# Pacing the scatters of the routing loop by value products, and fewer idle matmuls before the experts

## The chip, the cores and the metric

The kernel runs on one core of one Trainium2 chip. The metric is the device time of one launch in microseconds (us), the median of several runs. A profile of one execution gives, for each engine, when every instruction began and ended and what it waited for. The engines are TensorE (PE, its weight loads PEld), VectorE (DVE), ScalarE (ACT), GpSimd (POOL) and SyncE (SP, which issues most transfers).

## What is computed

Two transformer layers on an input of 8 samples x 512 tokens x 128 features, each with an attention part and a feed-forward part around which a layer norm and a modulation by a condition vector stand. What matters here is layer 0. Its attention goes through 16 heads of 8 features; its feed-forward part sends each token to 4 of 16 experts:

```python
logits = -dist2 + jnp.einsum('bld,ed->ble', x, rw) + rb
topv, topi = jax.lax.top_k(logits, TOP_K)          # 4 of 16 experts per token
w = jax.nn.softmax(topv, axis=-1)
hidden = jax.nn.gelu(jnp.einsum('bld,efd->blef', x, w1) + b1, approximate=False)
exp_out = jnp.einsum('blef,edf->bled', hidden, w2) + b2
fused = jnp.sum(w[..., None] * sel, axis=2)        # the 4 chosen, weighted
```

Every expert has a 128x512 and a 512x128 matrix. Layer 1 follows with another attention and a spiking feed-forward part; the change leaves both alone.

## The kernel before

**The loop over samples (`layer0_attention`).** The work on a sample is cut into a front (projections, and fifteen steps d = 1 to 15 of a recurrence) and a back (scores, softmax, value products). A pass of the loop does the back of sample b and the front of sample b + 1, and, from the second sample on, also the routing of sample b - 1. In the first pass (sample 0's back) there is no routing; then come six passes of one `Fori` loop on each engine, and a last one without a front.

The order of instructions on each engine is a string: `weave(order, b=..., f=..., r=...)` takes the next piece of the back for a `b`, of the front for an `f` and of the routing for an `r`. `ORDER_ROUTE` holds these strings for the six passes: `'pe'`, `'ve'`, `'act'` and `'po'`. An engine runs its instructions strictly in the order of its string, and waits at each for the semaphores that it needs.

**What POOL does in a pass.** Of the recurrence, step d is: VectorE multiplies (L831, L837, tiles `a_tU`, `a_txy`), TensorE sums over heads (L1121, L1129), VectorE multiplies the result (L850, L855), and POOL subtracts it from `a_K` (L456, one instruction) and `a_X` (L462, two). The next step needs these. The steps shrink: 128x480 elements at d = 1, 128x32 at d = 15.

In the routing of sample b - 1, `route_pool` issues sixteen scatters, one for each of 4 token tiles and 4 chosen experts (L1573): each writes 128 token rows of 130 numbers (67 KB) from `a_mats` to places in DRAM (`rows_h`) given by a list of indices. POOL issues them between the steps of the recurrence, where its string has an `r`.

**What TensorE does meanwhile.** The back's last part runs over 40 jobs (sample tile, head group, tile of keys): scores (L1301, L1310, L1313), an exponential on ScalarE (L664) and the value products (L1325, eight matmul instructions of one job in the trace). The event `e_pv` counts jobs whose value products are done: `e_pv(k)` is reached after job k.

**The end of a pass.** VectorE writes fourteen 128x512 products of the front to `a_mats` (L872). The tenth and later overwrite the rows that the scatters read, so ahead of them VectorE waits until all sixteen scatters have landed (`R.sent`). POOL waits for the same before it says that its pass is over. Then SyncE clears the semaphores and starts the next pass.

**The last routing and the experts (`layer0_experts`).** The routing of the last sample stands outside the loop. TensorE has six short pieces in it (`route_tensor`); between and behind them it runs idle matmuls (`warm`, L207: a 128x128 constant times itself into an unused bank; one `w` is one f32 matmul, which the trace shows as two matmul instructions). The string is `'w' * 7 + 'rwww' * 7 + 'w' * 80`. Meanwhile SyncE loads the weights of all experts (16 x 514 KB) and small tables, and POOL issues the last sixteen scatters.

Then 143 pages of 128 rows follow, each one expert's: SyncE waits until all scatters have landed (L1821) and loads page p from `rows_h` (L1826, 65 KB, up to ten ahead); TensorE transposes it (L1960), VectorE copies the transposed page (L1935), TensorE multiplies by the first matrix (L1968), ScalarE applies gelu (L1853), TensorE multiplies by the second (L1977), VectorE scales (L1943), POOL scatters the result (L1838). The product L1968 runs two pages behind L1960, and L1977 three. TensorE's instructions for the pages stand behind all idle matmuls.

## Time and profile before

| | us |
|---|---|
| median of 3 runs | 2345.96 |
| lowest and highest | 2341.86, 2352.36 |
| the profiled execution, time | 2352.26 |
| the profiled execution, span from first to last instruction | 2350.1 |
| TensorE busy | 2055.5 (87%) |
| VectorE busy | 1644.5 (70%) |
| ScalarE busy | 869.7 (37%) |
| GpSimd busy | 836.0 (36%) |
| mean granted TensorE clock | 0.903 (no unit) |

The profiled execution lies 6.3 us above the median and 2.16 us above its own span. A value of 1.00 for the granted clock means that TensorE ran at its higher level (2.4 GHz) all through a stretch, 0.50 that it ran at the lower one (1.2 GHz).

How to read it: the busy shares are an average over stages. The stages are, in us from the start of the span: set-up and sample 0's front to some 200; the back of sample 0 to 312 (its last value product); the six passes with routing, whose last value products end at 499.8, 687.5, 875.2, 1067.0, 1258.2 and 1449.3; the last back to 1645; the last routing to 1694; the expert pages to 1969; layer 1 to the end.

### The profile page before, as it was taken

The page shows a single profiled execution, that of the slowest core. Times are in us where ns is not written, and L with a number is a line of the kernel's source. Part 1 is how long each engine was busy: PE and PEld are TensorE (multiplying, and loading weights), DVE is VectorE, ACT ScalarE, POOL GpSimd, SP SyncE. Part 2 cuts the span into 40 slices and gives each one's busy share as a digit, 9 for nine tenths or more (in the row PEclk, how much of TensorE's full clock was granted, in tenths as well). Part 3 has the DMA queues.
Part 4 walks back from the last instruction along what each step waited for, and adds up shares of the span by engine and source line. Part 5 has one row for each costly group of instructions (what it writes and reads, how often), then busy time and mean ns, then how long its engine had stood idle before and what let it go on. Part 6 is the DMA issues. An engine that isn't in the chain of part 4 may idle for free. (4 is left out here: it accounts for less than half of the span.)

```text
span 2350.1 us, 44343 instructions
## 1 busy us (share of the span) xinstructions
PE 2055.5 (87%) x16519; PEld 1373.3 (58%) x16519; DVE 1644.5 (70%) x3673; ACT 869.7 (37%) x1694; POOL 836.0 (36%) x871
## 2 busy tenths in 40 slices
PE   4798998988988898898898899989799999788885
PEld 2573564564555465456456456766799998345443
DVE  5968759839938947856874883540366765999996
ACT  2022233223224234133222322312166653887782
POOL 1523413622532532451352254130366653222211
PEclk7898999989989989889898888987899999899997
DMA  3000000000000000000000000120622223100000
GB/s 108 10 3 15 1 2 15 11 12 15 4 19 15 1 20 17 1 20 3 14 13 10 15 4 18 37 97 1 238 72 72 72 71 90 49 18 28 5 9 14
DMA packets 70189, 72.63 MB, mean 31 GB/s; under 512 B 12976, under 2 KB 58592, under 8 KB 69840
## 3 DMA queue, kind: packets, MB, share of 16 engines
q1 hardware_dynamic: 61296, 51.75, 7.4%
q0 software_dynamic: 8672, 17.91, 2.2%
q8 instruction: 142, 2.33, 0.4%
q14 instruction: 79, 0.65, 0.1%
HBM read 38.05 MB, written 27.43 MB: 28 GB/s over the span
## 5 line engine op out<-in xcount | busy, mean ns | idle before, releaser
L664 ACT ACTIVATE a_prep<-ps 128x1536 f32<-128x1536 f32 (+1 forms) x112 | 155.6, 1389 | 349.8 <-PE ps L1310 207.3
L905 DVE TENSOR_REDUCE a_mpart<-ps 128x4 f32<-128x512 f32 x320 | 199.6, 683 | 56.8 <-PE ps L1251 33.7
L1853 ACT ACTIVATE b_hid<-ps,b_stage 128x128 f32<-128x128 f32 x572 | 162.8, 368 | 143.9 <-PE ps L1968 132.0
L1838 POOL DMA_INDIRECT rows_y<-b_orow,b_target x143 | 164.7, 1152 | 123.9 <-DVE b_orow L1943 120.6
L462 POOL TENSOR_TENSOR a_X<-a_X,a_txy 128x480 f32<-128x480 f32 (+14 forms) x240 | 180.9, 771 | 64.5 <-DVE a_txy L855 63.3
L456 POOL TENSOR_TENSOR a_K<-a_K,a_yU 128x480 f32<-128x480 f32 (+14 forms) x120 | 83.7, 697 | 331.0 <-DVE a_yU L850 329.8
L1129 PE MATMUL ps<-a_txy,cst 128*128 128x480 f32 (+14 forms) x480 | 181.7, 485 | 11.0 <-DVE a_txy L837 10.3
L1977 PE MATMUL ps<-b_stage,b_hid 128*128 128x128 f32 x1144 | 151.4, 276 | 1.5 <-ACT b_hid L1853 1.5
L1968 PE MATMUL ps<-b_hTp,b_stage 128*128 128x128 f32 x1144 | 151.2, 275 | 0.0
L207 PE MATMUL ps<-cst 128*128 128x128 f32 x862 | 133.7, 303 | 15.8 <-issue 10.3
L872 DVE TENSOR_TENSOR a_mats<-ps,cst 128x512 f32<-128x512 f32 x112 | 69.9, 684 | 100.9 <-PE ps L1158 100.9
L1977 PEld LDWEIGHTS ps<-b_stage,b_hid 128*128 128x128 f32 x1144 | 139.3, 192 | 2.0 <-ACT b_hid L1853 2.0
L207 PEld LDWEIGHTS ps<-cst 128*128 128x128 f32 x862 | 119.8, 212 | 33.9 <-issue 30.7
L1968 PEld LDWEIGHTS ps<-b_hTp,b_stage 128*128 128x128 f32 x1144 | 139.0, 192 | 0.0
L1573 POOL DMA_INDIRECT rows_h<-a_mats,r_slot x112 | 111.1, 992 | 72.4 <-DVE a_mpart L905 47.9
L1121 PE MATMUL ps<-a_tU,cst 128*128 128x480 f32 (+14 forms) x240 | 92.3, 469 | 41.0 <-DVE a_tU L831 40.6
L1129 PEld LDWEIGHTS ps<-a_txy,cst 128*128 128x128 f32 x480 | 86.4, 216 | 67.9 <-issue 40.1
L837 DVE TENSOR_TENSOR a_txy<-a_bw,a_X 128x480 f32<-128x480 f32 (+14 forms) x240 | 110.8, 484 | 20.7 <-POOL a_X L462 20.4
L855 DVE TENSOR_TENSOR a_txy<-a_wf,ps 128x480 f32<-128x480 f32 (+14 forms) x240 | 94.7, 416 | 40.4 <-PE ps L1129 39.6
L1247 PE MATMUL ps<-a_aux_g,a_g_hotb 24*128 24x512 bf16 (+1 forms) x320 | 94.9, 415 | 27.2 <-DVE a_mpart L905 20.9
L1325 PE MATMUL ps<-a_prep,a_values 128*32 128x128 f32 x2560 | 116.8, 306 | 1.7 <-issue 1.7
L1325 PEld LDWEIGHTS ps<-a_prep,a_values 128*32 128x32 f32 x2560 | 69.4, 120 | 64.9 <-issue 56.0
(467 smaller groups left out, 4578.5 us busy)
## 6 DMA issues: line engine op xcount, KB each, us to landing
b_hrow<-rows_h SPq DMA_DIRECT2D x143, 65.0 KB
b_w<-in_wexp SPq DMA_DIRECT2D x16, 514.0 KB
d_got<-rows_y SPq DMA_DIRECT2D x32, 256.0 KB, 4.0
rows_h<-a_txy SPq DMA_DIRECT2D x19, 325.0 KB
rows_y<-b_orow,b_target POOLq DMA_INDIRECT x143
out<-xs SPq DMA_DIRECT2D x8, 256.0 KB, 2.3
cst<-in_const SPq DMA_DIRECT2D x1, 1865.5 KB, 15.0
rows_h<-a_mats,r_slot POOLq DMA_INDIRECT x112
```

Of the source, the lines that this page charges most:

```text
L207: nc.tensor.matmul(out, square, square, start=True, stop=True, skip_group_check=True)
L462: nc.gpsimd.tensor_tensor(x, x, yX[:, a, 0:n].rearrange("p (c s) -> p c s", c=NC), ALU.subtract).then_inc(e_uX.sem, 1)
L664: nc.scalar.activation(Pt[:, at:at + width, :], ps[:, 4:4 + width, :], ACT.Exp).then_inc(e_exp.sem, width)
L837: nc.vector.tensor_tensor(by_chunk(tX[:, a, 0:n]), chunks(bw[:, :])[:, :, left], chunks(X2[:, a, :])[:, :, right], ALU.mult).then_inc(e_tX ...
L905: nc.vector.tensor_reduce(mpart[:, i, j, 4 * g:4 * g + 4], ps[:, 4 + n % 4, :].rearrange("p (r j) -> p r j", r=4), AX.X, ALU.max).then_inc ...
L1129: mm(ps[:, 1 + a, 0:n], con("block8"), tX[:, a, 0:n], start=True, stop=True).then_inc(e_pX.sem, 1)
L1325: last = mm(ps[32 * r:32 * r + 32, 7, 128 * g:128 * g + 128], vflat[:, v0:v0 + 32], Pt[:, at, 128 * r:128 * r + 128], start=j == i and g = ...
L1573: nc.gpsimd.indirect_dma_start(hrows, bass.IndirectOffsetOnAxis(R.slot[:, t, k:k + 1], 0), R.htok[:, t, k, :], None).then_inc(R.scattered, 16)
L1838: nc.gpsimd.indirect_dma_start(yrows, bass.IndirectOffsetOnAxis(target[:, p % DEEP:p % DEEP + 1], 0), orow[:, p % DEEP, :], None).then_inc ...
L1853: last = nc.scalar.activation(hid[:, p % 2, f, :], ps[:, p % 2, 128 * f:128 * f + 128], ACT.Gelu, bias=stage[:, p % 3, AT_B1 + f:AT_B1 + f ...
L1968: last = mm(ps[:, q % 2, 128 * f:128 * f + 128], stage[:, q % 3, 128 * f:128 * f + 128], hTp[:, q % 2, :], start=True, stop=True, skip_gro ...
L1977: last = mm(ps[:, 4 + r % 2, 0:D], hid[:, r % 2, f, :], stage[:, r % 3, F + D * f:F + D * f + D], start=f == 0, stop=f == NF - 1, skip_gro ...
```

## The change

Two edits. In the loop, `route_pool` gets a list of sixteen events: scatter n now also waits for `e_pv(2 * n + 1)`, the value products of job 2n + 1. With it POOL's string is another. Behind the last routing, 24 idle matmuls stand in place of 80.

```diff
@@ ORDER_ROUTE @@
-    'po': ('bbbbbbbfffffffffffffffbfffbfbbbfbbfbbffffffffffffrfrffrfrffrfrffrfrrfffrrrrrr'),
+    'po': ('bbbbbbbfffffffffffffffbfffbfbbbfbbfbbffffffffffffrfffrrfffrrffrfrfrffrfffrrrrrrr'),
@@ layer0_attention, POOL @@
-                both(b + 2, ORDER_ROUTE, b, r=route_pool(nc, po, R, V, hrows))
+                both(b + 2, ORDER_ROUTE, b, r=route_pool(nc, po, R, V, hrows, pace=[e_pv(2 * n + 1) for n in range(16)]))
@@ layer0_experts, TensorE @@
-            weave('w' * 7 + 'rwww' * 7 + 'w' * 80, r=route_tensor(nc, pe, ps, cst, R, V), w=warm(nc, ps[:, 7, 0:128], ident))
+            weave('w' * 7 + 'rwww' * 7 + 'w' * 24, r=route_tensor(nc, pe, ps, cst, R, V), w=warm(nc, ps[:, 7, 0:128], ident))
```

`route_pool` itself is unchanged; it already waits for `pace[4 * t + k]` ahead of each scatter where a list is given, as in the pass behind the loop.

On POOL, in a pass of the loop, from the first scatter on. L1573 is a scatter, L456 and L462 are the recurrence's subtractions (128x32xN is step 16 - N). Before:

```order
L1573 DMA rows_h<-a_mats,r_slot 77824x130
L456 TENSOR_TENSOR a_K<-a_K,a_yU 128x32x5
L1573 DMA rows_h<-a_mats,r_slot 77824x130
L462 TENSOR_TENSOR a_X<-a_X,a_txy 128x32x5 x2
L1573 DMA rows_h<-a_mats,r_slot 77824x130
L456 TENSOR_TENSOR a_K<-a_K,a_yU 128x32x4
L1573 DMA rows_h<-a_mats,r_slot 77824x130
L462 TENSOR_TENSOR a_X<-a_X,a_txy 128x32x4 x2
L1573 DMA rows_h<-a_mats,r_slot 77824x130
L456 TENSOR_TENSOR a_K<-a_K,a_yU 128x32x3
```

The same place after the change:

```order
L1573 DMA rows_h<-a_mats,r_slot 77824x130
L456 TENSOR_TENSOR a_K<-a_K,a_yU 128x32x5
L462 TENSOR_TENSOR a_X<-a_X,a_txy 128x32x5 x2
L1573 DMA rows_h<-a_mats,r_slot 77824x130 x2
L456 TENSOR_TENSOR a_K<-a_K,a_yU 128x32x4
L462 TENSOR_TENSOR a_X<-a_X,a_txy 128x32x4 x2
L1573 DMA rows_h<-a_mats,r_slot 77824x130 x2
L456 TENSOR_TENSOR a_K<-a_K,a_yU 128x32x3
```

At steps 11 and 12 the two subtractions from `a_X` now stand ahead of the scatter that stood ahead of them. At the end of the list six scatters stood behind the last step of the recurrence before, and seven stand there now. The other engines' lists are the same in the loop.

On TensorE, behind the last routing (L1764 is the last piece of the routing, L1960 the first transposes of pages), the difference of the two programs:

```order
 L207 MATMUL ps<-cst 128x128 x3
 L1764 MATMUL ps<-b_b,b_flat 128x128 x4
-L207 MATMUL ps<-cst 128x128 x86
+L207 MATMUL ps<-cst 128x128 x30
 L1960 MATMUL ps<-cst,b_hrow 128x128 x3
 L1968 MATMUL ps<-b_hTp,b_stage 128x128 x4
```

Six of the 86 come from the pieces `www` of the string, so 30 are left in place of 86, and nothing else moves.

## Rows read from the trace of the kernel before

**Rows 1.** Busy time by stretch: engines, granted clock, DMA share, GB/s; passes of the loop.

```profile
687.50:875.20 187.70, 166.97 (x1529) 102.14 (x1529) 135.87 (x310) 55.93 (x84) 72.55 (x83) 0.91 0.04 12
875.20:1067.00 191.80, 171.29 (x1529) 104.24 (x1529) 135.78 (x310) 55.82 (x84) 72.92 (x83) 0.88 0.04 11
...
687.50:816.30 128.80, 109.75 (x837) 67.57 (x838) 109.76 (x224) 37.05 (x68) 47.23 (x46) 0.92 0.03 8
875.20:1008.00 132.80, 114.05 (x838) 69.51 (x838) 109.59 (x224) 37.05 (x68) 47.42 (x46) 0.88 0.03 8
```

**Rows 2.** Timeline of POOL in the sixth pass: start, us, instruction, idle time before.

```profile
1412.73 0.87 POOL L462 TENSOR_TENSOR a_X<-a_X,a_txy 128x128 f32<-128x128 f32 x2
...
1419.04 0.98 POOL L1573 DMA_INDIRECT rows_h<-a_mats,r_slot  x1 [0.17 <-issue]
...
1432.80 0.96 POOL L1573 DMA_INDIRECT rows_h<-a_mats,r_slot  x1 [0.31 <-issue]
1462.09 0.61 POOL L465 COPY a_vown<-a_vf 128x512 f32<-128x512 f32 x1 [28.33 <-SPq L404]
```

**Rows 3.** Timeline of VectorE in the same pass.

```profile
1413.23 0.67 DVE L837 TENSOR_TENSOR a_txy<-a_bw,a_X 128x96 f32<-128x96 f32 x2 [1.38 <-POOL a_X L462]
...
1453.53 1.89 DVE L872 TENSOR_TENSOR a_mats<-ps,cst 128x512 f32<-128x512 f32 x3 [1.56 <-PE ps L1158]
```

**Rows 4.** Timeline of TensorE in the same pass.

```profile
1415.64 0.42 PE L1325 MATMUL ps<-a_prep,a_values 128*32 128x128 f32 x8
...
1425.98 0.39 PE L1301 MATMUL ps<-a_aux_g,a_aux_l 32*128 32x512 bf16 x3 [1.09 <-ACT a_prep L664]
...
1429.81 1.51 PE L1325 MATMUL ps<-a_prep,a_values 128*32 128x128 f32 x24
...
1435.40 1.51 PE L1325 MATMUL ps<-a_prep,a_values 128*32 128x128 f32 x24
...
1438.96 0.86 PE L1325 MATMUL ps<-a_prep,a_values 128*32 128x128 f32 x24
```

**Rows 5.** Busy time by stretch again: behind the last routing, and the pages.

```profile
1700.00:1950.00 250.00, 249.10 (x2234) 248.91 (x2233) 175.43 (x542) 149.69 (x527) 151.90 (x132) 1.00 0.25 71
1660.90:1669.70 8.80, 8.80 (x78) 8.79 (x78) 3.21 (x16) 0.00 (x0) 6.19 (x7) 1.00 1.02 407
1669.70:1684.30 14.60, 4.38 (x15) 3.09 (x14) 1.45 (x2) 0.00 (x0) 9.24 (x10) 0.62 0.98 338
1684.30:1694.50 10.20, 10.16 (x81) 10.15 (x81) 0.00 (x0) 0.00 (x0) 0.00 (x0) 0.88 0.21 48
```

**Rows 6.** Timeline behind the last routing, 1660 to 1696 us, all engines.

```profile
1680.73 0.96 POOL L1573 DMA_INDIRECT rows_h<-b_htok,r_slot  x1 [0.31 <-issue]
...
1695.27 0.30 PE L1960 MATMUL ps<-cst,b_hrow 128*128 128x128 f32 x1 [0.37 <-DVE b_hTp L1935]
...
1695.41 1.12 PE L1968 MATMUL ps<-b_hTp,b_stage 128*128 128x128 f32 x8
```

**Rows 7.** Timeline of SyncE's queue between 1684 and 1700 us.

```profile
1685.99 10.17 SPq L1826 DMA_DIRECT2D b_hrow<-rows_h  x10
```

**Rows 8.** Busy time by stretch of 1 us while the first pages land.

```profile
1686.00:1687.00 1.00, 1.00 (x7) 1.00 (x7) 0.00 (x0) 0.00 (x0) 0.00 (x0) 0.61 0.11 21
1687.00:1688.00 1.00, 1.00 (x11) 1.00 (x11) 0.00 (x0) 0.00 (x0) 0.00 (x0) 1.00 0.26 61
...
1689.00:1690.00 1.00, 1.00 (x11) 1.00 (x11) 0.00 (x0) 0.00 (x0) 0.00 (x0) 1.00 0.32 67
```

**Rows 9.** The idle matmuls (L207) between 1660.9 and 1694.6 us: count, durations in ns.

```profile
L207 PE MATMUL ps<-cst x172: 268/276/556, 1660.9 to 1694.4; 128*128 128x128 f32 x172
```

**Rows 10.** Another start of TensorE after a pause, at layer 1: timeline, then busy time.

```profile
1976.30 11.69 PE L207 MATMUL ps<-cst 128*128 128x128 f32 x88 [3.28 <-PEq L1773]
```

**Rows 11.** Busy time by stretch: the start of that burst.

```profile
1976.90:1980.30 3.40, 3.40 (x18) 3.40 (x18) 1.14 (x1) 1.44 (x5) 0.00 (x0) 0.50 0.95 269
```

**Rows 12.** DMA queues between 1660 and 1663 us: packets, MB, share of 16 engines.

```profile
q8 instruction: 1, 0.02, 2.1%
```

More of the change, by code:

```diff
@@ L163 @@
            'rffbffrffrfffffffbfffffffffffffffffffffbffffffffffffffbbbbbbfffbbbfffbb'),
-    'po': ('bbbbbbbfffffffffffffffbfffbfbbbfbbfbbffffffffffffrfrffrfrffrfrffrfrffrrfffrrrrrr'),
+    'po': ('bbbbbbbfffffffffffffffbfffbfbbbfbbfbbffffffffffffrfffrrfffrrffrfrfrffrfffrrrrrrr'),
 }
```

## Prediction

> **What bounds the kernel now.** I read the page's busy shares first: TensorE is busy for 87% of the span and its granted clock averages 0.903. So in most stages TensorE's own list sets the pace, and an engine beside it can be late without cost. Then I read the two places that the change touches.
>
> In the loop, the busy times by stretch [rows 1] show two kinds of pass. From the last value product of one sample to that of the next it takes 187.7 us in the second and third pass and 191.8, 191.2 and 191.1 in the next three. The scores and value products, which are the part with the scatters, take the same in both kinds: 875.2 - 816.3 = 58.9 us and 1067.0 - 1008.0 = 59.0. The rest takes 128.8 or 132.8 us, at a granted clock of 0.92 or 0.88. So the 3.5 us between the kinds lie outside the part with the scatters and are clock. In that part TensorE is all but never idle: its longest pause in the sixth pass is 1.09 us, and ScalarE's exponential ends it, not POOL or VectorE [rows 4].
>
> Behind the last routing, the stretches [rows 5] show three phases of TensorE: dense idle matmuls to 1669.7, then 14.6 us in which only 15 matmuls and 14 loads ran while the DMA engines were full (0.98), then 81 dense ones to 1694.5. The first pages stand behind them, and the pages are bound by TensorE from there on: 249.1 us busy in 250.
>
> **The loop, part by part.** A scatter costs POOL 0.96 to 1.0 us, before and after; nothing is added there but sixteen waits in POOL's queue. Scatter n waits for job 2n + 1. What is queued behind a waiting scatter is the next subtraction of the recurrence, for which VectorE and then TensorE wait.
>
> Do the waits hold? The tightest of the scatters between the steps is the eighth. It starts at 1419.04 [rows 2], and its job 15 is the eight products that begin at 1415.64 and end at 1416.06 [rows 4]: 3.0 us in hand. The others of the first twelve have 3 us or more. From the thirteenth on the waits do hold: jobs 25, 27, 29 and 31 lie in the groups of three jobs (24 products each) that end at 1431.3, 1436.9 and 1439.8 [rows 4]. The last scatter moves from 1432.80 [rows 2] to about 1439.7, which is 6.9 us. Behind these four POOL has nothing to do: they are the last of its pass, and it then stands idle for 28.33 us until the next pass at 1462.09 [rows 2].
>
> Who waits for their landing? VectorE before the tenth product into `a_mats`, the second of the three from 1453.53, so 1454.2 [rows 3]. The landing itself: where the DMA engines were full, a scatter begun at 1680.73 [rows 6] was down when SyncE went on at 1685.99 [rows 7], 5.3 us; in the loop, with a DMA share of 0.04 [rows 1], it should be less. 1439.7 + 5.3 = 1445.0 leaves 9 us. Cost: 0, and if that cover were gone, what is later than 1454.2 would count in full, six times.
>
> The moved order gives something back off the path: at step 12 the subtractions from `a_X` stood behind a scatter, began at 1412.73 [rows 2], and VectorE stood idle 1.38 us for them [rows 3]; step 11 is alike. They now go first, about 1 us earlier. TensorE was not waiting for it, since its list was full there, so I count 0. The bounds: nothing below, and 1 us for each of two places in six passes, 12 us, if TensorE did feel them; I take 0, because its only pause over 1 us there has another cause [rows 4].
>
> **The idle matmuls.** 86 matmuls are 172 instructions [rows 9], 56 fewer matmuls are 112 fewer. Dense, one takes 8.80 / 78 = 0.113 us [rows 5], so the 60 that are left end at 1660.9 + 6.8 = 1667.7, before the thin phase begins. TensorE then waits for pages.
>
> The pages come as before, because SyncE's first load does not depend on TensorE: it goes out at 1685.99, the ten within 10.17 us [rows 7]. The stretches of 1 us [rows 8] show 61 KB in 1687 to 1688 and 67 in 1689 to 1690, with the same between; a page is 65 KB, so three are down at 1690.0. The third transpose, from which the list of the pages runs without a gap, begins at 1695.27 with the first product at 1695.41 [rows 6]. It can begin at 1690.0: 5.3 us earlier.
>
> Off this goes the clock. Now the idle matmuls raise it before the pages: their second burst starts at 1684.34 and the stretch 1686 to 1687 has 0.61, which is the lower level until 1686.8, so 2.4 us into the burst [rows 8]. At layer 1 a burst that starts at 1976.30 after a pause of 3.28 us runs at 0.50 up to 1980.3 at least, 4.0 us [rows 10, 11]. After the change the pages themselves are that burst. At the lower level TensorE does half, so 2.4 to 4.0 us cost 1.2 to 2.0. If the gaps of a starting pipeline kept the level low for 8 us it would be 4.0; if TensorE were not slowed at all, 0. I take 1.6, the middle of the two measured starts.
>
> The sum: 5.3 - 1.6 = 3.7 us, between 1.3 and 5.3. It passes whole through the pages, which TensorE bounds. The profiled execution should come from 2352.26 (span 2350.1) to 2348.6 (2346.4); that execution is 6.3 us above the median, and against the median it is 2345.96 - 3.7 = **2342.3 us**.
>
> The Trainium skill, in "TensorE: Matmul & The Clock Gate", section "What's actually happening", says that the throttled state is the default and that activity releases it. That rule speaks against this edit, since idle matmuls are such activity; by itself it gives the 1.2 to 2.0 us that the rows above have, and no more.
>
> **Rivals.**
>
> *The thin phase exists only under the profiler.* For it: in the 14.6 us TensorE took an instruction every 0.5 us (15 and 14, rows 5), while POOL went on issuing a scatter every 1.3 us, and a block of TensorE's instructions came in during the full phase of the DMA engines [rows 12]. So neither a lack of instructions nor of data explains it. Without the thin phase the 172 instructions end at 1660.9 + 172 x 0.113 = 1680.3, 8 us before the first page, and the 56 matmuls were free in every timed run. Then the time is 2345.96, no change, and only the profile gets shorter. Against it: the phase begins and ends with the DMA load (338 GB/s, then 48), and the profiled execution is no slower than the slowest timed one (2352.26 against 2352.36).
>
> The Trainium skill has two rules on this. "NOTIFIC — the notification-queue block", section "Overflow: three behaviours, one of which stalls the engine", says that the block which writes trace records holds its producer up rather than lose a record inside it. "Runtime: NRT & Kernel Launch", section "Instruction fetch mechanics", says that TensorE holds 2048 instructions, refilled in blocks of 256. Both are for this rival; no row here shows either.
>
> *The loop's passes change their kind for the better.* Three of six profiled passes are of the long kind. All six at 187.7 would take 4.1 + 3.5 + 3.4 = 11.0 us off the profiled execution; but the median is already 6.3 below it, so about 4.7 are left: 2342.3 - 4.7 = 2337.6. For it: VectorE's work moves by a microsecond in each pass. Against: that is not where the kinds differ [rows 1].
>
> *The passes go to the long kind.* The mechanism is the clock in the front's part of a pass: 132.8 in place of 128.8 us, at 0.88 [rows 1]. All six long are 6 x 3.5 = 21 us above all short, the median is 4.7 above all short, so 16.3 are left to lose: 2342.3 + 16.3 = 2358.6, slower than before. It decides when one more stretch of a pass falls to the lower level, as it did from the fourth pass on with no change at all in the program.
>
> *A paced scatter holds up the recurrence.* That needs the value products to come 3.0 us later against POOL's list than now [rows 2, 4]. Every further microsecond then delays a subtraction and TensorE behind it in six passes: at 2 us over, 12 us, 2354. Nothing moves TensorE's list in the loop, so this is unlikely.
>
> **How the numbers follow.** Forecast 0.45 (2340.7 to 2344.7); thin phase only under the profiler 0.32 (2346); short passes 0.11; long passes 0.08; held recurrence 0.04. The runs before lie 10.5 us apart, which is three passes of the other kind, so each case is blurred by some 4 us. A range of 2336 to 2352 leaves out the last two cases and the far end of the short passes, about 2 in 10. A measurement tells some 0.5% from no change, 11.7 us: faster than 2334.2 needs short passes and more, 0.07; slower than 2357.7 is the upper end of the long passes, 0.05; within it 0.88.
>
> **What would show it.** In the profile after: 60 idle matmul instructions behind the last piece of the routing, ending near 1667.7 on the old scale, no thin phase, the first transposes 6 us nearer to the routing's end than now (1688 on the old scale), a low clock at the first two pages. In the loop: the last scatter some 7 us later, VectorE's waits for `a_X` of 1.4 us gone, the value part still 58.9 us. I am wrong if the pages start later than 3 us before their old place, if the value part changes, or if VectorE waits for landed scatters. If the profile gains 3.7 us and the timed runs nothing, the first rival has it.

## The result, and the profile after

The changed kernel takes 2376.4 us (median of 4, 2364.4 to 2383.5) against 2344.6 for the kernel before in the same comparison (median of 4): ratio 1.0125, 95% interval 1.0073 to 1.0177. It is slower by 1.2%, where 2342.3 us and no measurable change were forecast. The profiled execution takes 2383.5 us with a span of 2381.4, 31.3 more than before. (Ratios leave out runs over 1.5% above the fastest of their kernel and medians keep them, which shows in e9, where one of four is left out, and in e16, three of ten.)

From the page of the changed kernel, the row of busy times:

```profile
PE 2068.6 (87%) x16407; PEld 1370.8 (58%) x16407; DVE 1648.6 (69%) x3673; ACT 871.1 (37%) x1694; POOL 836.6 (35%) x871
```

TensorE has 112 instructions fewer and is busy 13.1 us longer. The mean granted clock of the profiled execution is 0.889 (0.903 before).

**The loop.** Busy time by stretch of the changed kernel, with the columns of [rows 1]: the third of the six passes, its front's part, its part with scores and value products, and a piece of that.

```profile
700.10:900.60 200.50, 179.02 (x1529) 108.48 (x1529) 136.60 (x310) 55.94 (x84) 72.92 (x83) 0.85 0.04 11
700.10:831.10 131.00, 111.22 (x834) 67.89 (x838) 109.90 (x224) 37.07 (x68) 47.28 (x46) 0.91 0.03 8
831.10:900.60 69.50, 67.80 (x707) 40.58 (x695) 26.71 (x87) 18.87 (x16) 25.64 (x38) 0.73 0.05 17
...
854.60:888.70 34.10, 34.10 (x282) 21.06 (x282) 4.76 (x20) 9.29 (x7) 12.89 (x20) 0.50 0.06 20
```

The same 1529 matmuls now take 200.5 us, against 187.7 or 191.8 in [rows 1]. The front's part, 131.0 us, lies between the two known lengths (128.8 and 132.8); the value part, the scores and value products, took 58.9 us in every pass before and has grown by ten. In one piece of 34.1 us TensorE is busy without a gap, but at a granted clock of 0.50. (Below, a value part is counted from the start of its first product: 59.5 us for each pass before.) The six value parts of the changed kernel take 60.7, 64.4, 69.8, 69.8, 69.9 and 59.5 us: 37.4 more in all. The front's parts take 5.4 more. The last sample, whose code is unchanged, gives 9.4 back, again by the clock. The first of these rows is the kernel before, the second the one after:

```profile
1449.30:1636.10 186.80, 168.37 (x1627) 121.27 (x1623) 68.57 (x165) 44.20 (x62) 36.21 (x37) 0.86 0.12 43
```

```profile
1492.20:1669.60 177.40, 162.28 (x1624) 117.19 (x1623) 68.32 (x165) 44.23 (x62) 36.28 (x37) 0.89 0.13 45
```

What stands ahead of the low clock, in the sixth pass of the changed kernel: the timelines of TensorE, ScalarE and POOL (start, us, instruction, idle time before).

```profile
1449.56 1.43 PE L1310 MATMUL ps<-a_shared,a_roll_k 32*16 32x64 f32 x42
1450.92 0.96 PE L1325 MATMUL ps<-a_prep,a_values 128*32 128x128 f32 x22
1452.17 0.40 PE L1325 MATMUL ps<-a_prep,a_values 128*32 128x128 f32 x2 [0.29 <-issue]
...
1454.51 0.39 PE L1301 MATMUL ps<-a_aux_g,a_aux_l 32*128 32x512 bf16 x3 [1.07 <-ACT a_prep L664]
```

```profile
1453.01 1.45 ACT L664 ACTIVATE a_prep<-ps 128x1536 f32<-128x1536 f32 x1 [4.74 <-PE ps L1325]
```

```profile
1450.15 1.05 POOL L1573 DMA_INDIRECT rows_h<-a_mats,r_slot  x1 [0.16 <-issue]
1451.51 0.96 POOL L1573 DMA_INDIRECT rows_h<-a_mats,r_slot  x1 [0.30 <-issue]
```

The exponential waits for the matmuls L1310, which end at 1450.99; it begins 2.0 us after that. (The view names L1325, whose matmuls had ended when the report came; the step of L1310's own semaphore is recorded 1.94 us behind the last of them. Such a step, by which an engine tells the others that it is done, is called a report below.) In those 2 us stand two scatters in a row, which the new order has at step 11. TensorE halts 0.29 us in the middle of the value products, for nothing that the profile shows, and then 1.07 us for the exponential. The pause of 1.09 us in [rows 4] is the same thing. The rows of ScalarE and POOL around it, in the kernel before:

```profile
1424.48 1.45 ACT L664 ACTIVATE a_prep<-ps 128x1536 f32<-128x1536 f32 x1 [3.78 <-PE ps L1325]
```

```profile
1421.63 0.99 POOL L1573 DMA_INDIRECT rows_h<-a_mats,r_slot  x1 [0.16 <-issue]
1422.92 0.96 POOL L1573 DMA_INDIRECT rows_h<-a_mats,r_slot  x1 [0.30 <-issue]
```

The L1310 of these jobs end at 1422.50, so this exponential too is 2.0 us late, and here it is the ninth and tenth scatter that stand in a row. The pause ends 34.6 us into the value part in the first three passes and 36.1 in the last three. After the change it ends at 20.4 to 24.5 us. Behind the second pair of the new order, at step 12, TensorE does not halt; in the first and the last pass a further pause of 0.94 us ends 48 to 49 us into the value part, among the last scatters.

**POOL and VectorE.** The last scatter of the sixth pass, and what follows on POOL; then VectorE's first product on `a_X` at step 13:

```profile
1482.79 0.96 POOL L1573 DMA_INDIRECT rows_h<-a_mats,r_slot  x1 [1.47 <-PE ps L1325]
1504.95 0.61 POOL L465 COPY a_vown<-a_vf 128x512 f32<-128x512 f32 x1 [21.21 <-SPq L404]
```

```profile
1455.11 0.68 DVE L837 TENSOR_TENSOR a_txy<-a_bw,a_X 128x96 f32<-128x96 f32 x2
```

The waits hold from the thirteenth scatter on, and POOL still stands idle for 21.21 us behind them (28.33 in [rows 2]). VectorE no longer waits for `a_X` here (1.38 us in [rows 3]); over the whole kernel these waits of L837 sum to 3.2 us in place of 20.4. The products into `a_mats` wait for TensorE's L1158 (1.56 us ahead of the three from 1496.40, as in [rows 3]), and not for scatters.

**The pages.** TensorE behind the last routing, then the clock at the first pages:

```profile
1693.36 6.96 PE L207 MATMUL ps<-cst 128*128 128x128 f32 x60
1722.37 0.45 PE L1960 MATMUL ps<-cst,b_hrow 128*128 128x128 f32 x1 [22.05 <-DMA b_hrow<-rows_h]
...
1724.42 0.47 PE L1960 MATMUL ps<-cst,b_hrow 128*128 128x128 f32 x1 [0.56 <-DMA b_hrow<-rows_h]
1724.68 1.91 PE L1968 MATMUL ps<-b_hTp,b_stage 128*128 128x128 f32 x8
```

```profile
1722.30:1728.40 6.10, 4.91 (x21) 4.35 (x22) 1.68 (x7) 1.14 (x4) 0.00 (x0) 0.50 0.28 65
1728.40:1735.00 6.60, 6.60 (x61) 6.60 (x61) 4.29 (x14) 4.17 (x15) 3.43 (x3) 1.00 0.25 62
```

In both programs one can count from the end of the routing's matmuls: the third transpose comes at 31.0 us against 34.3 before, the last at 298.7 against 300.6: 1.9 us gained.

### The profile page after: what moved, and what is told of

It is laid out like the page before. It is cut to its first block and busy times, and to the rows that moved or that the text cites. A ratio compares the mean times of both kernels' runs of the same rounds, so it can differ in the third digit from the quotient of the medians.

```text
span 2381.4 us, 44119 instructions
## 1 busy us (share of the span) xinstructions
PE 2068.6 (87%) x16407; PEld 1370.8 (58%) x16407; DVE 1648.6 (69%) x3673; ACT 871.1 (37%) x1694; POOL 836.6 (35%) x871
## 5 line engine op out<-in xcount | busy, mean ns | idle before, releaser
L456 POOL TENSOR_TENSOR a_K<-a_K,a_yU 128x480 f32<-128x480 f32 (+14 forms) x120 | 83.7, 698 | 371.0 <-DVE a_yU L850 370.1
L462 POOL TENSOR_TENSOR a_X<-a_X,a_txy 128x480 f32<-128x480 f32 (+14 forms) x240 | 181.6, 772 | 83.8 <-DVE a_txy L855 82.0
L1129 PE MATMUL ps<-a_txy,cst 128*128 128x480 f32 (+14 forms) x480 | 187.9, 500 | 13.8 <-DVE a_txy L837 13.0
L1573 POOL DMA_INDIRECT rows_h<-a_mats,r_slot x112 | 110.7, 988 | 101.3 <-DVE a_mpart L905 47.0
L872 DVE TENSOR_TENSOR a_mats<-ps,cst 128x512 f32<-128x512 f32 x112 | 69.9, 683 | 104.0 <-PE ps L1158 104.0
L1325 PE MATMUL ps<-a_prep,a_values 128*32 128x128 f32 x2560 | 123.0, 316 | 1.8 <-issue 1.7
L207 PE MATMUL ps<-cst 128*128 128x128 f32 x750 | 115.1, 299 | 5.4 <-PEq L1773 3.2
L207 PEld LDWEIGHTS ps<-cst 128*128 128x128 f32 x750 | 102.1, 207 | 23.4 <-issue 20.2
L837 DVE TENSOR_TENSOR a_txy<-a_bw,a_X 128x480 f32<-128x480 f32 (+14 forms) x240 | 110.3, 482 | 3.5 <-POOL a_X L462 3.2
L1325 PEld LDWEIGHTS ps<-a_prep,a_values 128*32 128x32 f32 x2560 | 72.1, 123 | 67.4 <-issue 56.6
```

What stands on the lines that cost most here:

```text
L207: nc.tensor.matmul(out, square, square, start=True, stop=True, skip_group_check=True)
L462: nc.gpsimd.tensor_tensor(x, x, yX[:, a, 0:n].rearrange("p (c s) -> p c s", c=NC), ALU.subtract).then_inc(e_uX.sem, 1)
L837: nc.vector.tensor_tensor(by_chunk(tX[:, a, 0:n]), chunks(bw[:, :])[:, :, left], chunks(X2[:, a, :])[:, :, right], ALU.mult).then_inc(e_tX ...
L1129: mm(ps[:, 1 + a, 0:n], con("block8"), tX[:, a, 0:n], start=True, stop=True).then_inc(e_pX.sem, 1)
L1325: last = mm(ps[32 * r:32 * r + 32, 7, 128 * g:128 * g + 128], vflat[:, v0:v0 + 32], Pt[:, at, 128 * r:128 * r + 128], start=j == i and g = ...
L1573: nc.gpsimd.indirect_dma_start(hrows, bass.IndirectOffsetOnAxis(R.slot[:, t, k:k + 1], 0), R.htok[:, t, k, :], None).then_inc(R.scattered, 16)
```

## The experiments

Each of the five groups of experiments ran on one chip, another for each group, and before was timed beside it. Theory 1 was that scatters in a row make reports between engines late, that TensorE pauses for it, and that the clock goes down after a pause there. Rivals: the waits in POOL's queue, the missing idle matmuls, the chip, chance.

### The parts alone (e1 to e4)

e1_idle24:

```diff
-            weave('w' * 7 + 'rwww' * 7 + 'w' * 80, r=route_tensor(...
+            weave('w' * 7 + 'rwww' * 7 + 'w' * 24, r=route_tensor(...
```

> The kernel before with twenty-four idle matmuls in place of eighty behind the last routing, and nothing else; the loop is as before. In the profile after, the pages' first transpose stands 29.0 us behind the start of the last row of idle matmuls (1693.36 to 1722.37) against 33.6 us before (1660.9 to 1694.5), and the last transpose 298.7 against 300.6 us: 1.9 us earlier. If the pairs of scatters or the waits in the loop made the changed kernel slower, this one is 1 to 4 us faster than before (ratio 0.998 to 1.000), with passes of 187.7 and 191 us. If the idle matmuls keep the clock up for what follows, it carries part of the loss: 2350 to 2376. If the thin phase exists only under the profiler, the profiled span is 2 to 4 us shorter and the timed runs do not move.

e2_order (the changed string of POOL, without waits):

```diff
-    'po': ('...ffffffffffffrfrffrfrffrfrffrfrffrrfffrrrrrr'),
+    'po': ('...ffffffffffffrfffrrfffrrffrfrfrffrfffrrrrrrr'),
```

> The kernel before with the changed order of the scatters in the loop alone; no scatter waits for value products, eighty idle matmuls. Theory 1 (pairs): a scatter that starts right behind another holds up the reports between the engines for some 2.4 us, TensorE pauses and ScalarE's exponential begins 2 us late; the new order makes such pairs at the steps 11 and 12, some 13 us earlier in the value part, and the clock falls there. Then this kernel carries all or most of the loss: value parts of 64 to 69 us in place of 58.9, passes of 198 to 201, time 2370 to 2385. Theory 2 (waits): the loss comes from scatters that stand in POOL's queue waiting, or land late; then this kernel takes 2340 to 2350. Theory 3 (both needed): in between, 2350 to 2368.

e3_waits (the waits, with the string of before):

```diff
-                both(b + 2, ORDER_ROUTE, b, r=route_pool(nc, po, R, V, hrows))
+                both(b + 2, ORDER_ROUTE, b, r=route_pool(nc, po, R, V, hrows, pace=[e_pv(2 * n + 1) for n in range(16)]))
```

> The kernel before with the sixteen waits on value products alone; the order of the scatters is that of before. The waits bind from the thirteenth scatter on. Theory 1 (pairs): the only pair between the steps is the one of before (the ninth and tenth), so nothing is lost: 2338 to 2352, perhaps a little less, since the row of six at the end is spread out. Theory 2 (waits): it carries the loss, 2370 to 2385. A mixture of both gives 2352 to 2368.

e4_apart (no scatter behind another between the steps; at the end of the list the eleventh and twelfth still begin 1.3 to 2.1 us apart):

```diff
-    'po': ('...ffffffffffffrfrffrfrffrfrffrfrffrrfffrrrrrr'),
+    'po': ('...ffffffffffffrfrffrfrffrfrffrfrffrfrffrrrrrr'),
...
+                ... pace=[e_pv(n) for n in (1, 1, 1, 1, 1, 1, 1, 1, 1, 1, 1, 24, 27, 30, 33, 36)]))
```

> The kernel before with no two scatters in a row: the tenth goes behind the subtraction of step 15, and the last five wait for the value products of jobs 24, 27, 30, 33 and 36; eighty idle matmuls. Theory 1 (pairs): the pause of the value products with the ninth and tenth scatter (0.28 us inside a group, then 1.09 us before the scores) goes, and with it the fall of the clock behind it; the value part comes under 58.9 us, by 1.4 us at least in each of six passes and by up to 5 us if the clock stays up for the 10 to 14 us that it is down now: 2315 to 2338. Theory 2 (waits): it has as many binding waits as the changed kernel and loses as much: 2365 to 2385. If the clock's pattern comes of other things, value parts stay at 58.9 and the time at 2340 to 2350.

Measured, against 2308.4 us for before (31 runs, 2286.8 to 2335.8): e1 2306.9, ratio 1.0018 [0.9976, 1.0060]; e2 2309.1, 0.9996 [0.9954, 1.0038]; e3 2309.5, 1.0013 [0.9965, 1.0062]; e4 2312.7, 1.0014 [0.9971, 1.0056]. No part moves the time, and keeping scatters apart gains nothing either. The times of 2338 us and more that the theories gave are all missed, because before itself is 36 us faster here than in the first comparison, which I had not expected. The value part of e2, with the pairs of the changed order in it, and one of e4:

```profile
1187.20:1243.40 56.20, 55.81 (x708) 33.94 (x707) 27.31 (x88) 18.86 (x16) 25.75 (x38) 0.91 0.07 21
```

```profile
1189.30:1241.00 51.70, 51.11 (x708) 31.70 (x707) 26.73 (x87) 18.76 (x16) 25.28 (x38) 1.00 0.07 21
```

e2 shows no pause behind its pairs. 51.7 us is what a value part takes if the clock never falls. So either order and waits are slow only together, or the chip is a condition. The parts were not run again on a chip like that of the first comparison.

### The whole change on another chip (e5 to e8)

e5_before is the kernel before, e6_changed the changed kernel, e7_loop the changed loop with eighty idle matmuls. e8_late:

```diff
-    'po': ('...ffffffffffffrfrffrfrffrfrffrfrffrrfffrrrrrr'),
+    'po': ('...fffffffffffffffffffffffffffrrrrrrrrrrrrrrrr'),
```

> The kernel before once more, unchanged, for a profile of it beside those of the changed parts on the same chip. In the first comparison it took 2344.6 us and its value parts 59.4; among the runs of the parts it took 2308.4, and none of the four profiles there (e1 to e4) had a report of TensorE more than 1.0 us late, where the two first profiles had such in every pass (up to 1.9 us behind a pair of scatters). Theory 1 (the chip, not the program): here its value parts take 52 to 56 us and the scatters hold up no reports, if the time is near 2308; or 59.4 us with late reports, if it is near 2345. Theory 2 (chance of one execution): value parts of both kinds within runs of one call, and no link between late reports and time.

> The changed kernel, whole. Theory 1 (late reports behind pairs of scatters, on some chips alone): where before takes near 2308 us, it is 0 to 3 us faster than before or the same (ratio 0.997 to 1.001), with value parts of 52 to 56 us; where before takes near 2345 us, it is 1.2% slower again, with the pause of 1.1 us some 20 us into the value part. Theory 2 (the order and the waits together cost time on any chip, though neither does alone): 1.2% slower here too, 2330 to 2340 against 2308.

> The changed loop (order and waits) with the eighty idle matmuls of before. Theory 1: as the changed kernel in the loop, and 1.9 us slower than it behind the last routing. Where the changed kernel is 1.2% slower than before, this one is too, and the idle matmuls have no part in the loss; where it is not, this one is within 0.3% of before. If the idle matmuls were the cause, this kernel would be at before's time while the changed one is slower.

> The kernel before with all sixteen scatters of a pass behind the last step of the recurrence, in one row of some 20 us (from 1426 to 1447 on the scale of before), so that none lies in the first 36 us of the value part and fifteen stand right behind another. Theory 1, on a chip with late reports: the pause of 1.1 us at the ninth and tenth scatter goes, the first 36 us of the value part get shorter by 1.4 us or more, and late reports come in the row behind it; the time is 2320 to 2360 by how the clock takes it. On a chip without: the same as before within 0.3%, and no report late. If a row of scatters costs time on any chip, 10 us or more over before.

Measured, against 2309.5 (31 runs): e5 2311.6, 0.9974 [0.9940, 1.0008]; e6 2309.6, 0.9979 [0.9940, 1.0017]; e7 2307.8, 1.0003 [0.9963, 1.0042]; e8 2301.3, 0.9974 [0.9939, 1.0009]. The whole change makes no difference here, and sixteen scatters in one row (e8) cost nothing. From e6: the value part of the fifth pass by stretch, and in the sixth TensorE's L1310, the exponential of the same jobs as above and the pair of scatters.

```profile
1187.10:1243.10 56.00, 55.58 (x707) 33.77 (x699) 27.09 (x87) 18.86 (x16) 25.57 (x38) 0.91 0.07 21
```

```profile
1391.71 1.43 PE L1310 MATMUL ps<-a_shared,a_roll_k 32*16 32x64 f32 x42
```

```profile
1393.25 1.45 ACT L664 ACTIVATE a_prep<-ps 128x1536 f32<-128x1536 f32 x1 [2.84 <-PE ps L1310]
```

```profile
1392.32 1.05 POOL L1573 DMA_INDIRECT rows_h<-a_mats,r_slot  x1 [0.16 <-issue]
1393.67 0.96 POOL L1573 DMA_INDIRECT rows_h<-a_mats,r_slot  x1 [0.30 <-PE ps L1325]
```

The 42 matmuls L1310 end at 1393.14 here and the exponential begins 0.1 us later, with the same two scatters around it. So scatters in a row are not enough to make a report late. With each report of TensorE in the loop set against the end of its matmul, none of e1 to e15 is more than 0.3 us behind; in the first comparison L1310's is 1.9 us behind at this place in each of the six passes of both kernels. The page of e5 also shows which chip it is, in its list of transfers:

```profile
b_hrow<-rows_h SPq DMA_DIRECT2D x143, 65.0 KB, 1.9
b_w<-in_wexp SPq DMA_DIRECT2D x16, 514.0 KB, 10.2
```

The last number is the time from issue to landing. The pages of the first comparison have none for these two, because many landings are missing from those traces. Counted from the traces, 5053 and 5070 reports lie behind the last value product in before and after, and over 8600 in every trace of e1 to e15; in the front's parts, where nothing is scattered, the numbers are the same (916 in most). The time between the two kinds of chip lies in the same places. The span of before is 2350.1 us in the first comparison and 2310.2 in e5; of these 39.9 us, 29.6 are in the six value parts, 11.3 in the last sample and 5.1 between the routing's end and the last transpose of a page, while the front's parts are 5.8 us shorter in the first comparison.

And the idle matmuls in e5, from the end of the routing to the first page:

```profile
1627.34 19.47 PE L207 MATMUL ps<-cst 128*128 128x128 f32 x172
1654.14 0.45 PE L1960 MATMUL ps<-cst,b_hrow 128*128 128x128 f32 x1 [7.33 <-DMA b_hrow<-rows_h]
```

There is no thin phase. All 172 instructions are through in 19.47 us, and TensorE then waits 7.33 us for the page. In e1 to e15 the last transpose comes 295.3 to 297.0 us behind the routing, with either number of idle matmuls.

### A pause made on purpose (e9 to e12)

Is the pause the cause of the low clock, or another sign of the chip? e9_late12 makes it on a chip without late reports:

```diff
+        aside = sb("aside", [128, 6, 208], BF16)
...
                     at, width = LANES * (k % 2), len(group)
+                    if k in late:
+                        for n in range(6):
+                            nc.scalar.activation(aside[:, n, :], ps[:, 4, 0:208], ACT.Exp)
                     nc.scalar.activation(Pt[:, at:at + width, :], ps[:, 4:4 + width, :], ACT.Exp).then_inc(e_exp.sem, width)
...
+                weave(order['act'], b=back((4,) if routing else ()), f=front(nxt, True), **routing)
```

e10_late24 has `(8,)` there. e11_changed_late12 is the changed kernel with `(4,)`, and e12_changed the changed kernel.

> The kernel before, with six small activations on data nobody uses (some 1.8 us) ahead of ScalarE's exponential of the jobs 12 to 14 in the loop. In the changed kernel's first trace that exponential began 2 us late, TensorE stood 1.1 us for it some 22 us into the value part, and 1.8 us later its clock fell for 34 us; on the two chips of the runs e1 to e8 none of the three was there. Theory 1 (a pause of TensorE at this place makes the clock fall and stay low; where the pause comes from does not matter): the clock falls at 23 to 27 us into the value part for 17 to 34 us, value parts of 60 to 70 us in place of 53 to 56, 6 x 7 to 14 = 40 to 80 us over before. Theory 2 (the fall had another cause, such as the chip): the pause costs itself at most, 1 to 2 us a pass, 6 to 12 us over before (ratio 1.003 to 1.005), and the clock keeps its pattern.

> The same six activations ahead of the exponential of the jobs 24 to 26, where the first trace of the kernel before had the pause (34.6 us into the value part, and the clock fell there for 13.6 us; on the other chips it falls at the same place for 6.8 or 10.2 us, or not at all, without a pause). Theory 1: the value parts of the first trace of before come back, 58 to 60 us in every pass, 20 to 35 us over before (ratio 1.009 to 1.015), and less than e9. Theory 2: 6 to 12 us.

> The changed kernel with the six activations ahead of the exponential of the jobs 12 to 14. Theory 1: as e9, value parts of 60 to 70 us. If the new order of the scatters behind the pause is what holds the clock low, it is above e9 by 10 us or more; if the pause alone does it, within 8 us of e9. Theory 2: 6 to 12 us over the changed kernel.

> The changed kernel once more, beside the other three, for a third chip if it is one. On a chip like those of e1 to e8 (before near 2308 us, no report over 1 us late) the ratio to before is 0.994 to 1.002; on one like the first (before near 2345, reports up to 1.9 us late behind a pair of scatters) it is 1.007 to 1.018 again. If the ratio of the first comparison was chance, it is near 1.000 even where before takes 2345.

Measured, against 2313.0 (19 runs): e9 2351.3 (4 runs), 1.0118 [1.0029, 1.0206]; e10 2336.1, 1.0112 [1.0077, 1.0147]; e11 2342.1 (4 runs), 1.0111 [1.0024, 1.0197]; e12 2308.1, 0.9955 [0.9911, 0.9999]. In e9, fourth pass, TensorE, ScalarE (L667 is the added work; lines are shifted by 4), and busy time by stretch:

```profile
1033.10 0.86 PE L1329 MATMUL ps<-a_prep,a_values 128*32 128x128 f32 x24
...
1036.15 0.39 PE L1305 MATMUL ps<-a_aux_g,a_aux_l 32*128 32x512 bf16 x3 [1.32 <-ACT a_prep L668]
```

```profile
1033.22 1.52 ACT L667 ACTIVATE a_aside<-ps 128x208 bf16<-128x208 f32 x6 [2.78 <-PE ps L1314]
1034.58 1.51 ACT L668 ACTIVATE a_prep<-ps 128x1536 f32<-128x1536 f32 x1
```

```profile
1016.30:1084.00 67.70, 66.07 (x708) 40.12 (x707) 26.61 (x88) 20.28 (x22) 25.96 (x38) 0.74 0.06 17
...
1037.30:1071.40 34.10, 34.10 (x277) 20.53 (x277) 5.45 (x23) 8.36 (x7) 14.78 (x22) 0.50 0.08 25
```

That is the picture of the changed kernel's first trace, on a chip where no report is late and with the order of before: a pause of 1.32 us at 20 us, the clock down 1.1 us behind its end, and down for 34.1 us. In all twelve passes of e9 and e11 the clock falls 1.1 to 3.4 us behind the end of this pause; in no pass of the traces of e1 to e8 does it fall between 11 and 34 us into the value part. How long it stays down differs, from 3.4 to 34.2 us, and what decides it is open. The changed kernel's first trace has both as well: down behind the pause for 17.1 us in one pass and 34.1 in three, and for 3.4 and 6.8 us in the first and the last. Where it is long, the value part takes 7 to 17 us more than the 52.9 to 56.1 of e5. The value parts of the traces, in us, with the time at the lower clock in brackets (worked out from the clock's changes in each trace):

```text
before, 1st comparison  59.5 59.5 59.5 59.4 59.4 59.4   (14 14 14 14 14 14)
after, 1st comparison   60.7 64.4 69.8 69.8 69.9 59.5   (10 24 38 38 38  7)
e5_before               56.1 52.9 52.9 52.9 56.1 56.1   (11  4  4  4 10 10)
e6_changed              56.3 56.1 56.1 56.2 56.2 56.2   (11 10 10 10 10 10)
e9_late12               67.9 56.0 63.5 67.7 63.4 70.4   (35  7 24 35 24 38)
e10_late24              59.0 57.5 58.9 62.8 59.8 59.0   (14 11 14 20 17 14)
e11_changed_late12      56.2 55.9 56.2 69.1 58.8 67.8   ( 7  7  7 34 10 35)
```

e10, with the pause where before had it, gives nearly the value parts of before's first trace. Its ratio says the same as e9's within the intervals; in the profiled executions the early pause is the dearer one (the six value parts sum to 327.0 us in e5, 357.0 in e10 and 388.9 in e9), but the profiled execution of e9, 2365.0 us, is the longest of its four, and the timed runs do not separate the two. Theory 1 had forecast 40 to 80 us for e9; the medians differ by 38 and the ratio says 27, so it is between the two theories in size. e11 lies no higher than e9 (337.0 in e6, 364.0 in e11), so the new order adds nothing to the pause. Theory 1's second half stands in kind: a pause of 1.3 us at this place is enough to make the clock fall. The Trainium skill says in "TensorE: Matmul & The Clock Gate", section "What's actually happening", that activity releases the throttle; the traces agree (a clock of 0.50 up to 3.7 us behind the first product of the pages, and 1.00 from there), and show beside it that a TensorE busy all the time can stay at 0.50 for 34.1 us.

### Looking for the first kind of chip (e13 to e18)

e13_changed and e16_changed are the changed kernel, e14_order is e2, e15_waits is e3. e17_late12_half is e9 with `range(3)`, e18_late18 is e9 with `(6,)`.

> The changed kernel on one more chip. If reports come late behind pairs of scatters here (before near 2345 us, value parts of before 59.4 us), ratio 1.007 to 1.018 and the clock low for 34 us in the value parts; if not (before 2300 to 2315), 0.994 to 1.002 and value parts of 52 to 56 us, low for 0 to 11 us.

> The changed order of the scatters alone. With late reports: as the changed kernel in the value parts (60 to 70 us), ratio 1.007 to 1.02, since the pair at step 11 is in the order. If the waits were needed for the loss: ratio near 1.00 with value parts of 59.4. Without late reports: ratio 0.995 to 1.005.

> The waits alone, with the order of before. With late reports: value parts as before, 59.4 us, ratio 0.997 to 1.003, since the only pair between the steps is that of before. If the waits bring the loss: 1.007 to 1.02. Without late reports: ratio 0.995 to 1.005.

> The changed kernel on one more chip. Without late reports: ratio to before 0.995 to 1.003, value parts of 52 to 56 us, before at 2300 to 2315. With late reports: 1.007 to 1.018, before near 2345.

> The kernel before with three small activations (0.9 us) in place of six ahead of the exponential of the jobs 12 to 14. TensorE's pause there should be 0.3 to 0.5 us in place of 1.3. If the clock needs a pause of 1 us to fall, it keeps its pattern: value parts of 52 to 57 us, ratio 0.998 to 1.003. If any pause at this place makes it fall: value parts of 60 to 70 in some passes, ratio 1.005 to 1.015.

> The kernel before with the six activations ahead of the exponential of the jobs 18 to 20, between the places of e9 and e10, some 28 us into the value part. If the clock goes by the pause wherever it lies, as e9 and e10: value parts of 58 to 70 us, ratio 1.008 to 1.015. If the pause must meet an already thin stretch of TensorE, it costs itself alone: 53 to 58 us, ratio 1.000 to 1.005.

Measured, e13 to e15 against 2306.3 (25 runs): 2310.7, 1.0002 [0.9965, 1.0038]; 2313.0, 1.0022 [0.9984, 1.0059]; 2306.5, 1.0026 [0.9985, 1.0066]. A fourth chip without late reports, and no difference.

The last group met the first kind (it may be the chip of the first comparison itself). Before takes 2342.9 us there (19 runs, 2329.4 to 2362.9). e16 takes 2369.4 (2337.3 to 2400.3), medians 1.1% apart, and 1.0051 [0.9993, 1.0109] by the ratio, which does not rule out no change. Its page has no landing times, and 5034 reports behind the last value product:

```profile
b_hrow<-rows_h SPq DMA_DIRECT2D x143, 65.0 KB
b_w<-in_wexp SPq DMA_DIRECT2D x16, 514.0 KB
```

The timelines of POOL and TensorE in its sixth pass, and the value part:

```profile
1431.07 1.05 POOL L1573 DMA_INDIRECT rows_h<-a_mats,r_slot  x1 [0.16 <-issue]
1432.42 0.96 POOL L1573 DMA_INDIRECT rows_h<-a_mats,r_slot  x1 [0.30 <-issue]
```

```profile
1430.46 1.43 PE L1310 MATMUL ps<-a_shared,a_roll_k 32*16 32x64 f32 x42
1431.82 0.96 PE L1325 MATMUL ps<-a_prep,a_values 128*32 128x128 f32 x23
1433.08 0.28 PE L1325 MATMUL ps<-a_prep,a_values 128*32 128x128 f32 x1 [0.30 <-issue]
...
1435.41 0.39 PE L1301 MATMUL ps<-a_aux_g,a_aux_l 32*128 32x512 bf16 x3 [1.18 <-ACT a_prep L664]
```

```profile
1413.40:1483.20 69.80, 67.96 (x708) 40.92 (x707) 27.04 (x88) 18.86 (x16) 25.90 (x38) 0.73 0.05 17
1437.20:1471.30 34.10, 34.10 (x283) 21.03 (x282) 4.76 (x20) 9.29 (x7) 12.82 (x20) 0.50 0.06 20
```

Everything of the first trace is back. Its six value parts take 65.7, 59.6, 57.8, 64.1, 69.8 and 69.8 us (27, 7, 7, 24, 38 and 38 at the lower clock).

e18, on the same chip, has the order of before: its pair of scatters stands 14.5 us later in the value part, and so does the halt. POOL and TensorE, fifth pass:

```profile
1222.87 0.98 POOL L1577 DMA_INDIRECT rows_h<-a_mats,r_slot  x1 [0.16 <-issue]
1224.16 0.96 POOL L1577 DMA_INDIRECT rows_h<-a_mats,r_slot  x1 [0.30 <-issue]
```

```profile
1223.91 0.66 PE L1329 MATMUL ps<-a_prep,a_values 128*32 128x128 f32 x13
1224.87 0.43 PE L1329 MATMUL ps<-a_prep,a_values 128*32 128x128 f32 x6 [0.30 <-issue]
1225.60 0.44 PE L1329 MATMUL ps<-a_prep,a_values 128*32 128x128 f32 x5 [0.30 <-issue]
```

So on one chip the halt stands behind the first pair of scatters of either order, at step 11 or step 14. The six value parts sum to 386.9 us in e16 and 355.9 in e18 (356.8 in the first trace of before), so that the changed order has 31 us more on the same chip. e18's own delay (a pause of 0.74 us at 28 us) costs nothing: 2338.9, 0.9975 [0.9942, 1.0008], and no fall of the clock follows it ahead of the one behind the pair. e17 takes 2364.8 (4 runs), 1.0111 [1.0030, 1.0192]. Half the delay makes a pause of 0.61 us there, at 19 to 23 us. In the last three passes the clock falls 1.8 to 3.3 us behind it, for 13.6 to 34.2 us, and the value parts take 65.9 to 67.0; in the third it falls for 3.4 us; in the first two it does not fall behind it. So a short pause is not harmless, as one of my two forecasts for e17 had it. Whether 28 us is a harmless place anywhere, or on this kind of chip alone, e18 cannot tell, since it ran on this kind only.

On this chip the thin phase is back in e17 and e18, which have eighty idle matmuls. e18:

```profile
1653.00:1667.00 14.00, 4.94 (x22) 3.65 (x21) 1.52 (x2) 0.00 (x0) 9.70 (x11) 0.68 1.03 373
```

Its last transpose comes 300.8 us behind the routing, e17's 300.5, and e16's, with the twenty-four, 296.5: 4.0 to 4.3 us earlier.

## Why the prediction was wrong

**The waits of the scatters and their landing** went as worked out: they hold from the thirteenth on, nobody waits for it (POOL idle for 21.21 us behind the last one in the sixth pass), and e3 and e15 cost nothing measurable, on chips without late reports.

**The order** is the step that failed. I wrote that TensorE was not waiting, since its list was full there, and counted 0, with 0 and a gain of 12 us as bounds; a loss was not among them. I had the row that spoke against it, the pause of 1.09 us in [rows 4], and set it aside as ScalarE's: "its only pause over 1 us there has another cause". I did not ask why ScalarE was late. TensorE's reports to it came late behind two scatters in a row, and the new order makes such a pair 14 us earlier. On chips of that kind the pause itself costs little, since it was there before. What it costs is clock: the six value parts of the profiled execution take 37.4 us more, and have 154 us at the lower level in place of 84. If TensorE does half its work there, those 70 us are 35 of the 37.4, which is an estimate. That it was the order and not the waits rests on the traces: the pause ends at 20.4 to 24.5 us, and no scatter is held by value products before the thirteenth, 44 us or more into the value part. No run had the order alone on a chip of this kind. I had named a change of the value part as a sign of being wrong, and that sign came. The rival on the long kind of passes had the mechanism, the clock, and its rule (one more stretch at the lower level), but looked for it in the front's part, and at 3.5 us a pass; the stretch found is 34.1 us long and costs 10.

**The idle matmuls.** The step was right in kind on the first kind of chip: 1.9 us in the first comparison and about 4.2 on the chip of e16 to e18, against 3.7. The cold start took what I gave it (0.50 until 1728.4, 3.7 us behind the first product, so 1.9). The term that was mis-sized is the earlier pages: 34.3 - 31.0 = 3.3 us in the first comparison, where I had 5.3 (less the 1.9 this gives 1.4, and the last transpose gained 1.9); against e17, e16's third transpose comes 5.8 us earlier (28.4 against 34.2). On four chips there is no thin phase and the cut is worth nothing (e1, 1.0018). That was the rival "only under the profiler", with the wrong condition: not profiler or not, but the kind of chip; whether the writing of trace records has a part in it, no run here tells, since each timed run has a span and a granted clock of its own on record and none is known to be without a recorder. I had also ruled out a lack of instructions by [rows 12]; that row shows one packet of instructions and not whose, so it rules out nothing. The Trainium skill, "NOTIFIC — the notification-queue block", section "Overflow: three behaviours, one of which stalls the engine", says that a full queue of that block drops the new record, overwrites the oldest or stalls its producer, by how it is set. Missing records and halts without a cause, on the same chips and in the same stretches, would be two of these at once, at different places of the block; no run shows it.

**The range.** It was built from the spread of three runs of one kernel on one chip. On the four other chips the whole change and its parts are within 0.5% of before; the forecast of no change holds there and fails where it was to be measured.

**What stays open.** Why one chip, or two, makes reports late around scatters, and whether a kernel with its scatters kept apart (e4) is faster there: it ran on a chip of the other kind alone. Whether the order alone is slower there, since e2 and e14 ran on chips of the other kind. And how much of the 1.2% is robust there: the first comparison has 1.0073 to 1.0177, the second 0.9993 to 1.0109.

## What to carry to other kernels

A pause that the profile puts down to another engine has to be followed one step further before it is called unrelated: to what made that engine late, and to what the change moves there. Where TensorE is the bound, a short pause can cost far more than itself: one of 0.6 to 1.3 us cost some 7 to 17 us of clock in some passes here and next to nothing in others. And a difference of 1% on one chip is worth a second chip: here the pages told the two kinds apart, by transfers without a landing time.

## What was not expected of the hardware

- Two kinds of chips: before takes 2343 to 2345 us (medians) in the first comparison and beside e16, and 2306 to 2313 on the four chips of e1 to e15.
- On the first kind a report of TensorE arrived 1.9 us late behind two scatters in a row (2.0 us from the last L1310 to the exponential, against 0.1 on the others, where no report in the loop is over 0.3 us late), and idle matmuls ran at one in some 0.6 us while the DMA engines were full (22 in 14.0 us, share 1.03), against 172 in 19.47 us at a share of 1.04.
- A TensorE busy for all of 34.1 us stayed at the lower clock (277 to 283 matmul instructions, mean clock 0.50).
- With the clock up all through, the value part takes 51.7 us; that is so in one pass of e4 and two of e15 (0 to 1 us at the lower level), and in no other trace.
